# Four elementwise products of a fused four-layer stack move from VectorE to GpSimd

## The reference: what is computed

```
ek = exp(min(k, 30));  ekv = ek * v
a  = a * decay + ekv_t;  b = b * decay + ek_t          # forwards (nf, df) and backwards (nb, db)
euk = exp(min(u + k, 30))
num = nf + nb - ekv + euk * v
den = df + db - ek + euk
y   = sigmoid(x) * num / max(den, 1e-8) * (0.8 + 0.2 * tf)
x   = x + ffn(y)
```

## Time and profile before

| | |
|---|---|
| median of 3 runs | 424.56 us (424.46 to 424.63) |
| span of the profiled execution, first to last instruction | 421.6 us |
| what lies around that span, by the median | 3.0 us |
| TensorE (PE) busy | 376.2 us, 89% of the span |
| VectorE (DVE) busy | 344.4 us, 82% |
| ScalarE (ACT) busy | 286.4 us, 68% |
| GpSimd (POOL) busy | 95.1 us, 23% |
| chain that ended last, by engine | PE 58%, DVE 25%, ACT 8%, issue 5%, DMA 2%, POOL 1% |

### The profile page before, as it was taken

The page is one execution under the profiler, slowest core; times in us unless marked ns, Lnnn a source line. Parts: engine busy times, 40 slices in busy tenths (PEclk is TensorE's granted clock), DMA queues, the critical chain, the costliest instruction groups (busy, mean ns, idle before and its releaser), DMA issues.

```text
span 421.6 us, 7295 instructions
## 1 busy us (share of the span) xinstructions
PE 376.2 (89%) x2609; PEld 322.3 (76%) x2609; DVE 344.4 (82%) x509; ACT 286.4 (68%) x506; POOL 95.1 (23%) x103
## 2 busy tenths in 40 slices
PE   2999577869887789999999999999999998999885
PEld 2998555649764469999999999999987687887543
DVE  4999878999875999999999980399703688799986
ACT  5996986886965278767576767666643345688873
POOL 4000121100030233353533322256641000000000
PEclk9999979999998989999999999999999999999999
DMA  7700000000058374731052168473001500000002
GB/s 278 249 0 2 1 2 0 0 2 2 0 150 296 80 240 158 233 111 40 30 174 99 37 237 301 180 241 141 26 14 61 166 0 2 0 2 0 2 26 76
DMA packets 22691, 38.55 MB, mean 91 GB/s; under 512 B 2088, under 2 KB 17080, under 8 KB 22528
## 3 DMA queue, kind: packets, MB, share of 16 engines
q1 hardware_dynamic: 17120, 24.98, 18.0%
q0 software_dynamic: 2528, 7.08, 5.1%
q10 hardware_dynamic: 3008, 6.03, 3.9%
HBM read 32.97 MB, written 5.11 MB: 90 GB/s over the span
## 4 chain that ended last, share of the span: by engine, by line
PE 58%; DVE 25%; ACT 8%; issue 5%; DMA 2%; POOL 1%; ACTq 0%; SPq 0%; DVEq 0%
PE bank L1775 20%; PE bank L1753 19%; PE bank L1573 3%; PE bank L1838 3%; PE bank L1828 2%; DVE scr L865 2%; DVE scr L867 2%; PE bank L1603 2%; DVE big L1265 1%; PE bank L1745 1%; DVE big L999 1%; PE bank L1634 1%; DVE small L1004 1%; PE bank L1639 1%; DMA v<-in_kT 1%
## 5 line engine op out<-in xcount | busy, mean ns | idle before, releaser
L1753 PE MATMUL bank<-big,yT 128*128 x368 | 83.3, 379 | 0.0
L620 ACT ACTIVATE yT<-bank,big 128x128 f32<-128x128 f32 x184 | 52.5, 369 | 42.6 <-PE bank L1775 42.4
L1753 PEld LDWEIGHTS bank<-big,yT 128*128 128x128 f32 x368 | 68.1, 190 | 8.7 <-issue 0.4
L377 POOL TENSOR_TENSOR small<-small 128x2 f32<-128x2 f32 (+1 forms) x9 | 11.5, 1276 | 167.0 <-DVE small L1300 71.1
L425 POOL DMA_INDIRECT choice_rows<-yo,rowo x23 | 33.3, 1449 | 62.7 <-ACT yo L629 48.3
L410 POOL DMA_INDIRECT xg<-token_rows,rowi x23 | 31.9, 1387 | 52.4 <-PE bank L1745 32.9
L1573 PE MATMUL bank<-identf,scr 128*128 128x128 f32 x240 | 30.7, 286 | 5.6 <-DVE scr L867 5.6
L1573 PEld LDWEIGHTS bank<-identf,scr 128*128 128x128 f32 x240 | 29.4, 201 | 6.2 <-DVE scr L867 6.1
L1775 PEld LDWEIGHTS bank<-ygT,big 128*128 128x128 f32 x256 | 29.8, 192 | 1.9 <-issue 1.6
L1775 PE MATMUL bank<-ygT,big 128*128 128x128 f32 x256 | 29.9, 275 | 1.4 <-ACT ygT L612 1.4
L1775 PEld LDWEIGHTS bank<-ygT,w3T 128*128 128x128 f32 x256 | 29.7, 192 | 1.2 <-issue 0.9
(11 more groups left out here) (370 smaller groups left out, 811.0 us busy)
## 6 DMA issues: line engine op xcount, KB each, us to landing
big<-in_moe_w SPq DMA_DIRECT2D x16, 1024.0 KB, 6.7
v<-in_kT SPq DMA_DIRECT2D x2, 512.0 KB, 4.5
big<-in_gateT SPq DMA_DIRECT2D x1, 1024.0 KB, 7.0
big<-in_upT SPq DMA_DIRECT2D x1, 1024.0 KB, 9.1
big<-in_downT SPq DMA_DIRECT2D x1, 1024.0 KB, 11.6
x<-in_x_bsc SPq DMA_DIRECT2D x1, 1024.0 KB, 13.8
token_rows<-y POOLq DMA_DIRECT2D x4, 256.0 KB, 7.7
ek<-in_w3a ACTq DMA_DIRECT2D x1, 1024.0 KB, 7.5
```

The lines of the kernel that those rows point to most:

```text
L620: ins = sc.activation(hT[j % 2][:, c], ps[1 + 2 * (j % 2) + c // 4][:, (c % 4) * P:(c % 4 + 1) * P], ACT.Gelu, bias=b1s[:, c, j:j + 1])
L1753: ins = te.matmul(ps[5 + 2 * (j % 2)][:, 0:C], hT[j % 2][:, c], big[:, bass.ds(at + (W2_AT + c * C), C)], start=(c == 0), stop=(c == IC - 1))
```

## The change

make_gv moves from VectorE's block into GpSimd's, with the same operands and waits. On GpSimd the first three products stand ahead of the first power, and the fourth between the second and the third power of the loop over pairs. VectorE's four calls go. Nothing else changes.

```diff
+            def make_gv(n):
+                pool.wait_ge(s["euk_ready"], n + 1)
+                if n >= 2:
+                    pool.wait_ge(s["num_ps"], 1 if n == 2 else 3)
+                gp.tensor_tensor(gv0[n], g[:, n // KC, n % KC], v[:, n % KC], ALU.mult).then_inc(s["gv0_ready"], 1)
+
+            for n in range(3):
+                make_gv(n)
             power(0, s["stat_tok"], 1, r_, ss, s["pow_ready"])
             for q in range(T // 2):
+                if q == 2:
+                    make_gv(3)
                 power(q, s["rms2_in"], q + 1, r_[:, 2 * q:2 * q + 2], ss[:, 2 * q:2 * q + 2], s["rms2_pow"])
...
-            def make_gv(n):
-                dve.wait_ge(s["euk_ready"], n + 1)
-                if n >= 2:
-                    dve.wait_ge(s["num_ps"], 1 if n == 2 else 3)
-                ve.tensor_tensor(gv0[n], g[:, n // KC, n % KC], v[:, n % KC], ALU.mult).then_inc(s["gv0_ready"], 1)
-
...
             make_ekv(0)
-            make_gv(0)
             sweep(0, False)
...
             floor_ps(0)
-            make_gv(1)
             sweep(1, False)
...
             q0T_of(3)
-            make_gv(2)
             dve.wait_ge(s["ld_x"], 16)
...
-                elif p == 1:
-                    make_gv(3)
                 dve.wait_ge(s["amax2"], 2 * p + 2)
```

## The result

The changed kernel takes 431.43 us (median of 4 runs, 430.31 to 435.72) where the kernel before takes 424.51 (4 runs): ratio 1.0173, 95% interval 1.0123 to 1.0223. So it is slower, as forecast, but by 6 to 7 us and not by 4.2, and outside the stated range.

The account below looks back on a forecast made before the run. VectorE, busy 38.13 of 38.50 us from 9.2 to 47.7, was taken as the bound. 3 x 1.86 + 0.92 - 2.29 = +4.21 us on the 421.6 span, plus the unchanged 3.0, gave 428.8 us; range 426.6 to 430.4.

Parts of the forecast that it names:

- VectorE as the bound up to 47.7 us: From 9.2 to 47.7 us VectorE is busy 38.13 of 38.50 us, so anything added or removed moves the end.
- the sign: Whole kernel: slower, by +4.21 us, with a chance of 0.88 for slower.
- The mechanism and its places: At all four products GpSimd and VectorE wait for each other's whole instruction: three delays of 1.86 us, one of 0.92.
- Rival 4: GpSimd waits for a real gap in VectorE's work, the first product ending at 26.7: +6.5 us, 431.1 us; chance 0.05.
- I take D = 2.12: Length of one 128x1024 GpSimd product alone, scaled from its 1280-column subtraction of 2.61 us: 2.12 us.
- "1.14 us" for gv0: First product, at 14.74 to 15.88 in VectorE's gapless stretch: removing it saves 1.14 us.
- TensorE's next matmuls and so on: After the second power, the fourth product delays VectorE's first small step by 0.92 us, passed on to gate product and TensorE.
- gv2 gives nothing: Third product: removing it from VectorE saves nothing, as the first gate product also waits for ScalarE's silu until 64.40.
- the power ends 0.90 earlier: Without the fourth product on VectorE, GpSimd's second power takes 0.70 instead of 1.60 us and ends at 83.54.
- nothing lost behind gv1 on TensorE: Second product: TensorE gets ek x v at about 18.5 instead of 17.5, which costs nothing more.
- The 3.0 us around the span: The median of the runs, 424.56, lies 3.0 us above the profiled span of 421.6; taken as unchanged.
- a shift that exists at 119 us arrives at the end whole: After about 120 us nothing of the change is left, so a delay present at 119 us reaches the end undiminished.

Follow-up runs that it names:

- the extra products: Kernel before plus three extra GpSimd products into a buffer nobody reads, VectorE keeping its own four: 433.00 against 425.06 us (1.0181).
- the memset: Kernel before plus three GpSimd memsets of 2048 columns, which only write, VectorE keeping its four products: 425.74 against 425.06 us (1.0015).
- the product behind the small steps: Kernel before with only the fourth product on GpSimd, waiting until VectorE's small steps after the second power are done: 424.24 against 425.06 us (0.9968).
- the gap is filled: Eight dummy matmuls before the seventh gate pair: changed kernel 430.30 against 431.86 us without; only the fourth product moved, 424.69 against 426.63 without.
- products 0 to 2: Changed kernel with the fourth product back on VectorE, the first three on GpSimd: 429.45 against 425.67 us for the kernel before (1.0085).
- product 3: Kernel before with only the fourth product on GpSimd, right behind the second power: 426.56 against 425.67 us, again 426.63 against 425.07.

## Why the prediction was wrong in size

- **VectorE as the bound up to 47.7 us, and the sign**: right. Every microsecond of hold-up in that stretch came out at the squares.
- **The mechanism and its places**: right at all four, shown by the extra products, the memset and the product behind the small steps. The Trainium skill's "SBUF — State Buffer", section "Who interferes with whom", says that a VectorE instruction with two SBUF inputs contends with a GpSimd instruction that reads SBUF, not with one that only writes, and not if it has at most one SBUF input, unless it runs in one of the modes that use both of VectorE's ports. The three runs agree: 4.39 us, 2.27 us, and 1.41 for two gate products.
- **Rival 4**: its 431.1 us lie nearest to the measured 431.43, but by chance. It had GpSimd wait for a real gap until 24.6 us; the row of the first product starts at 11.16 and ends at 13.67.
- **"I take D = 2.12"**: this step failed. The row it came from had a bf16 second operand (line 404 subtracts br, which line 114 makes bf16); I did not see it from the row, since the profile prints one input's type. With that type 1024 columns take 2.14, which is what I worked out; with two float32 operands 2.34. Each hold-up is then 2.12 instead of 1.86, and the fourth place costs 1.17 instead of 0.92: +1.0 us. The estimate of 2.25 from the Trainium skill's GPSIMD Engine Reference, section "Performance versus the Vector engine", which I set aside for the trace, was nearer.
- **"1.14 us" for gv0**: 0.19 too much. ek x v ends at 15.74 + 3.32 = 19.06, yet the next scan starts at 19.17, not 0.08 before that end. That scan reads the product, so it seems to wait for ek x v to be complete, and gv0 used to cover that wait; this is argued from the operands, no run tests it.
- **"TensorE's next matmuls and so on"**: this step failed too: a term was missing, and this is the part that only the runs show. The 0.92 was passed on to TensorE as a delay alone. But a gap of 1.8 us in front of these matmuls became 2.90 to 2.96, the clock fell in every one of four profiles, and 0.8 to 1.1 us were lost that come back when the gap is filled. What makes the clock fall at one gap and not at another is open: at the gap of 2.26 us it fell in some profiles only.
- **gv2 gives nothing, the power ends 0.90 earlier, nothing lost behind gv1 on TensorE**: as forecast (the power of 0.70 at 87.16; the early shift of 4.32 is 3 x 2.12 less 0.95 and 1.15, 4.26, within 0.1).
- **The 3.0 us around the span**: the runs listed with their spans lie 1.8 us above them (430.31 against 428.5). The profiled execution of before was about 1.1 us faster than the median, which I could not tell. It shifts no term of the sum.

Sum with the measured terms: 4.26 + 1.17 + 0.8 to 1.1 = 6.2 to 6.5, where the changed kernel has +6.2 beside the variants. Open is the difference between the parts and the whole: +3.8 for products 0 to 2 and +0.9 to +1.6 for product 3 make 4.7 to 5.4. The intervals allow both, and the kernel before loses some clock too in some of its executions, so a part of the 0.8 may not be new. Open are also the 0.6 us after 115 us in the first pair of profiles; so "a shift that exists at 119 us arrives at the end whole" held only within such scatter. The second profile of the changed kernel is 430.6 us long, 2.1 more than the first, though its fourth power starts only 0.29 later: from 340 to 345 us its granted clock is 0.66, in the first profile 1.00.

## What to carry to other kernels

A product moved from VectorE to GpSimd is off VectorE only if VectorE, while it runs, has no instruction that fetches two operands from SBUF; else VectorE stands still for nearly the whole of the slower engine's time (here 2.12 of 2.34 us). Two operands are not the only case. The instruction of 256 columns in the earlier trace rows has one tensor and a scalar for each partition as its inputs, and took 1.34 us behind GpSimd's copy. In the second profile of the kernel before it met no GpSimd instruction:

```profile
298.73 0.35 DVE L1216 TENSOR_SCALAR last_w<-big,last_g 128x256 f32<-128x256 f32 x1
```

So look for a stretch of instructions with a PSUM operand, as the gate products and sums here, and put the moved one there. And when a gap in front of TensorE gets longer, cost the matmuls behind it at the lower clock as well (here 3.1 to 3.5 us for eight instead of 1.89).

## What was not expected of the hardware

Two things were forecast, but from rows that did not show them directly: an instruction of 128x2 values is held up as long as one of 1024 columns, 2.23 us instead of 0.16, and GpSimd, waiting, gets its turn between two VectorE instructions that stand back to back, in each of the three early places, so a busy VectorE is no protection. Not forecast was that a bf16 second operand makes GpSimd's instruction of 1024 columns 0.20 us shorter (2.14 against 2.34), and that TensorE's clock at one and the same gap of 2.26 us fell in one of the two profiles of the kernel before and not in the other.
